# Sliding-window attention of a two-layer kernel: where in a quad the query, key and value pieces are projected and rotated

## The reference

```
h   = layernorm(x) * (1 + ca) + sa
xn  = h * rsqrt(mean(h * h) + 1e-6)
q, k, v = split(xn @ w_qkv.T)                # 16 heads of 64 each
q, k = apply_rope(q, cos, sin), apply_rope(k, cos, sin)
   # apply_rope: [x1 * c - x2 * s, x2 * c + x1 * s] on the two halves of a head
attn = softmax(where(mask, q @ k.T / 8, -1e9))   # mask: 0 <= q_pos - k_pos <= 32
x   = x + ga * ((attn @ v) @ w_out.T)
```

## Time and profile before

| what | value |
|---|---|
| median of 3 runs | 1284.41 us (1284.17 to 1285.26) |
| span of the profiled execution | 1295.1 us |
| PE busy | 975.8 us, 75% of the span |
| DVE busy | 805.3 us, 62% |
| ACT busy | 639.2 us, 49% |
| POOL busy | 430.4 us, 33% |

### The profile page before, as it was taken

The page is one execution under the profiler, slowest core; times in us unless marked ns, Lnnn a source line. Parts: engine busy times, 40 slices in busy tenths (PEclk is TensorE's granted clock), DMA queues, the critical chain, the costliest instruction groups (busy, mean ns, idle before and its releaser), DMA issues. The chain is left out here.

```text
span 1295.1 us, 25137 instructions
## 1 busy us (share of the span) xinstructions
PE 975.8 (75%) x8604; PEld 662.5 (51%) x8604; DVE 805.3 (62%) x1683; ACT 639.2 (49%) x2132; POOL 430.4 (33%) x332
## 2 busy tenths in 40 slices
PE   6779998989899999985613769747348787867665
PEld 3456565656656565664503556534225454545454
DVE  5777758687777767564657514112136878559995
ACT  3565767767676767671101323112038777643322
POOL 2334333333342423321000857886611312200221
PEclk9789899999999998987555789888759999868967
DMA  6564343434443434431402123445310000000000
GB/s 198 150 182 107 92 123 88 119 96 113 102 113 100 113 83 107 104 91 42 102 0 62 45 59 69 61 73 129 31 66 1 1 2 1 1 1 9 17 17 25
DMA packets 89009, 93.62 MB, mean 72 GB/s; under 512 B 18800, under 2 KB 62304, under 8 KB 88944
## 3 DMA queue, kind: packets, MB, share of 16 engines
q1 hardware_dynamic: 78576, 84.12, 24.7%
q0 software_dynamic: 10368, 8.66, 4.7%
HBM read 24.36 MB, written 10.70 MB: 27 GB/s over the span
## 5 line engine op out<-in xcount | busy, mean ns | idle before, releaser
L835 POOL TENSOR_TENSOR qk_cos<-qk_raw,const 128x512 f32<-128x512 f32 x128 | 183.2, 1432 | 313.0 <-ACT qk_raw L589 313.0
L575 ACT ACTIVATE prob<-psS,neg_max 128x96 f32<-128x96 f32 x512 | 167.9, 342 | 86.5 <-DVE neg_max L670 85.7
L442 PE MATMUL psQ<-a_xnT,weights 128*128 128x512 f32 x250 | 146.0, 668 | 2.1 <-ACT a_xnT L621 1.4
L550 PEld LDWEIGHTS psO<-probT,v_windows 96*64 96x64 f32 x2048 | 73.7, 143 | 142.6 <-ACT probT L649 121.1
L550 PE MATMUL psO<-probT,v_windows 96*64 96x64 f32 x2048 | 91.8, 235 | 43.9 <-ACT probT L649 43.9
L685 DVE TENSOR_TENSOR qk_roped<-qk_cos,qk_swapped 128x512 f32<-128x512 f32 x128 | 119.0, 929 | 5.9 <-DVE qk_swapped L676 5.5
L1508 POOL DMA_INDIRECT sums<-ex_y,ex_index x64 | 97.6, 1525 | 39.5 <-issue 23.5
L1497 POOL DMA_INDIRECT ex_rows<-rows,ex_index x64 | 67.1, 1048 | 121.8 <-DMA ex_index<-lists 102.6
L575 ACT ACTIVATION_READ_ACCUMULATOR prob<-psS,neg_max 128x1 f32 x512 | 105.4, 206 | 0.0
L1442 ACT ACTIVATE ex_hidden<-ex_psH,ex_b 128x512 f32<-128x512 f32 x64 | 43.7, 687 | 114.4 <-PE ex_psH L1401 59.7
L649 ACT COPY probT<-psT 96x512 f32<-96x512 f32 x128 | 76.8, 600 | 46.5 <-PE psT L530 46.5
(11 more groups left out here) (317 smaller groups left out, 1936.2 us busy)
## 6 DMA issues: line engine op xcount, KB each, us to landing
qk_swapped<-qk_raw SPq DMA_DIRECT2D x512, 64.0 KB, 2.0
v_windows<-v_tok SPq DMA_DIRECT2D x32, 384.0 KB, 4.4
v_windows<-v_tok SPq DMA_DIRECT2D x32, 256.0 KB, 3.6
mod<-mod_rows SPq DMA_DIRECT2D x12, 512.0 KB, 6.0
ex_w<-in_L_ffn_W SPq DMA_DIRECT2D x16, 256.0 KB
v_windows<-v_tok SPq DMA_DIRECT2D x32, 96.0 KB, 2.1
rows<-rt_h SPq DMA_DIRECT2D x8, 256.0 KB, 2.4
sums<-rt_zeros SPq DMA_DIRECT2D x8, 256.0 KB, 2.7
```

The lines of the kernel that those rows point to most:

```text
L442: last = nc.tensor.matmul(bank, k.wqkvT[:, col:col + P], xnT[:, :], start=True, stop=True)
L550: ins = nc.tensor.matmul(psO[D * j:D * j + D, i * P + a * HALF:i * P + (a + 1) * HALF], vw[:, par, a, t, hd], probT[:, 2 * j + i, a * HALF ...
L575: last = nc.scalar.activation(prob[:, s, 2 * j + i, :], psS[:, s, j, i * KW:(i + 1) * KW], ACT.Exp, bias=nmax[:, s, 2 * j + i:2 * j + i + ...
L835: nc.gpsimd.tensor_tensor(rcos[:, half, :], raw[:, half, :], k.const[:, K_COS:K_COS + T], ALU.mult).then_inc(cos_done, 1)
```

## The change

The six pieces of a quad are renumbered: 0 to 3 are the halves and 4 and 5 the value pieces. The plan's numbers stay, so that unit 2 now projects two halves and unit 3 two value pieces. A table, `ROPES`, says what DVE rotates: in unit 0 halves 2 and 3 of the next quad, both behind the sines of the first and the maxima, in unit 1 nothing, in units 2 and 3 as before. POOL and SP take the halves in the same order as before, with each one's wait set to its new place.

```diff
-        VALUE = (3, 5)
+        VALUE = (HALVES, HALVES + 1)
         PLAN = ((0,), (1,), (2, 3), (4, 5))
-        def half_of(m):
-            return m - m // 4
+        ROPES = (((1, 2), (1, 3)), (), ((2, 0),), ((2, 1),))
...
+        def ropes_at(u, last):
+            g, t = divmod(u, TILES)
+            return [(g + n, half) for n, half in ROPES[t] if not (last and g + n >= QUADS)]
...
                 for u in range(UNITS):
-                    t = u % TILES
-                    q, half = ahead(u, 6)
-                    roping = not (last and q >= QUADS)
+                    ropes = ropes_at(u, last)
                     if u > 0 and not (last and u + 1 >= UNITS):
                         divide(b, u + 1)
-                    if roping:
+                    for q, half in ropes[:1]:
                         done = sines(b, q, half)
-                    if t == 1 and roping:
-                        rope(b, q, half, done)
                     if not (last and u + 2 >= UNITS):
                         maxes(b, u + 2)
-                    if t != 1 and roping:
+                    for q, half in ropes[:1]:
                         rope(b, q, half, done)
+                    for q, half in ropes[1:]:
+                        rope(b, q, half, sines(b, q, half))
...
             def cosines(b, q, half):
-                first = isinstance(b, int) and b == 0 and q < 2
-                wait(pool, piece_out, b * QUADS * PIECES + q * PIECES + ((1, 2, 3, 4) if first else (1, 2, 3, 5))[half])
+                wait(pool, piece_out, b * QUADS * PIECES + q * PIECES + half + 1)
...
-                    q, half = ahead(u, 8)
-                    if not (last and q >= QUADS):
-                        swap(b, q, half)
+                    for q, m in pieces_at(g, t, last):
+                        if m not in VALUE:
+                            swap(b, q, m)
```

More of the change, by code:

```diff
@@ L357, in phase_attention0 @@
         ONTO = [psQ[:, 0, :], psQ[:, 1, :], psO[:, :]]
-        OPENING = [(0, m) for m in (0, 1, 2, 4, 3, 5)] + ["wo0", "wo1"] + [(1, m) for m in (0, 1, 2, 4, 3, 5)]
+        OPENING = [(0, m) for m in range(PIECES)] + ["wo0", "wo1"] + [(1, m) for m in range(PIECES)]
         scored, turned, applied = sem("scored"), sem("turned"), sem("applied")
@@ L391, in pieces_at @@
             return [] if last and g + 2 >= QUADS else [(g + 2, m) for m in PLAN[t]]
-        def ahead(u, n):
-            return (u + n) // HALVES, (u + n) % HALVES
+        def ropes_at(u, last):
+            g, t = divmod(u, TILES)
+            return [(g + n, half) for n, half in ROPES[t] if not (last and g + n >= QUADS)]
         def sixth_bank(n):
@@ L439, in project_onto @@
                 if m not in VALUE:
-                    half = half_of(m)
-                    col = (half % 2) * H0 * D + (2 * g + half // 2) * P
+                    col = (m % 2) * H0 * D + (2 * g + m // 2) * P
                     last = nc.tensor.matmul(bank, k.wqkvT[:, col:col + P], xnT[:, :], start=True, stop=True)
@@ L509, in _ @@
                     pe.wait_ge(w_dve, 1)
-                if OPENING[n] == (0, 3):
+                if OPENING[n] == (0, VALUE[0]):
                     pe.wait_ge(w_act, 2)
@@ L585, in piece_from @@
                 if m not in VALUE:
-                    half = half_of(m)
                     if not (isinstance(b, int) and b == 0 and q == 0):
-                        wait(act, roped, b * HALVES * QUADS + HALVES * (q - 1) + half + 1)
-                    ins = nc.scalar.copy(raw[:, half, :], bank)
+                        wait(act, roped, b * HALVES * QUADS + HALVES * (q - 1) + m + 1)
+                    ins = nc.scalar.copy(raw[:, m, :], bank)
                 else:
@@ L635, in _ @@
                 opening(n)
-                if OPENING[n] == (0, 4):
+                if OPENING[n] == (0, HALVES - 1):
                     copy_sixth(4)
@@ L843, in _ @@
             pool.wait_ge(ld_const, 16)
[L844 to L848, removed]
+            for q in range(2):
+                for half in range(HALVES):
+                    cosines(0, q, half)
             def body(b, last):
                 for u in range(UNITS):
-                    q, half = ahead(u, 7)
-                    if not (last and q >= QUADS):
-                        cosines(b, q, half)
+                    g, half = divmod(u, HALVES)
+                    if not (last and g + 2 >= QUADS):
+                        cosines(b, g + 2, half)
                     if u == 0 and isinstance(b, int) and b == 0:
@@ L867, in swap @@
             def swap(b, q, half):
-                first = isinstance(b, int) and b == 0 and q < 2
-                wait(sp, piece_out, b * QUADS * PIECES + q * PIECES + ((1, 2, 3, 4) if first else (1, 2, 3, 5))[half])
+                wait(sp, piece_out, b * QUADS * PIECES + q * PIECES + half + 1)
                 for n in range(4):
```

## The result

The changed kernel takes 1309.42 us (median; 1307.81 to 1309.57) where the kernel before takes 1284.84 beside it: ratio 1.0171, interval 1.0146 to 1.0196, slower by about 22 us (the two medians are 24.6 apart). The prediction was 1297 with a range up to 1306: right in direction, too small in size.

A forecast was written before the change was run, and what follows sets the result against it. No engine is full; waits going round between ACT, DVE and PE set a quad. Six sequences at 1.8 us (10.9), 1 for the first and 1.2 for the last give +13 us on 1284.4: 1297, range 1282 to 1306.

The forecast's parts named there:

- +0.35 into the third quad's unit 1: Delay carried through a sequence's first two quads to the third quad's unit 1, an estimate; bounds −0.4 and +1.4.
- +0.50 left in unit 0: Unit 0: part of unit 3's delay is covered by slack; exponentials start at 311.90 instead of 311.40.
- Unit 3's sines shut out: Unit 3: moved half's cosines meet the division and get in ahead of the sines; exponentials 1.02 us later.
- Two rotations in unit 0: End of unit 0: cosines shut out the first rope, two ropes queue, DVE 1.6 us late at unit 1.
- The division in unit 1: Unit 1: cosines ask 0.20 us ahead of the division and shut it out; exponentials 1.46 us later.
- the division wins: Rival in unit 1: division gets in ahead of the cosines; quad only 0.60 us longer, 1291 us; chance 0.25.
- What costs nothing: Items priced at zero: PE's 0.26 us wait for the rope goes, the late division follows; last half's swap has time.
- "worse" rival: Unit 2: a third meeting, cosines with its division, adds 0.57 us a quad; 1311 us; chance 0.05.
- first sequence: One more cosine ahead of the first sequence's loop; +1 us, bounds −1 and +3.
- six middle sequences: Each of six sequences 1.8 us longer, from +0.35 and the third quad's 1.46; 10.9 us together.
- last sequence: Last sequence, which projects in two quads only; +1.2 us.
- likeliest case: Both meetings happen, with unit 3's sines and unit 1's division shut out; 1297 us, 1292 to 1303; chance 0.45.

The follow-up runs named there:

- x4: Changed kernel with twelve dead transposes ahead of PE's wait for unit 1's division in the second and fourth quad; 1295.30 us, ratio 1.0066 to the kernel before.
- x3: Changed kernel, but POOL's cosines of the last half wait for unit 3's maxima; 1284.95 us, ratio 0.9985 to the kernel before.
- x5: Changed kernel, but POOL's cosines of half 1 wait for unit 1's division; 1292.18 us, ratio 1.0037 to the kernel before.
- x10: Kernel before with the same twelve dead transposes at the same two places; 1285.18 us, ratio 0.9996 to the kernel before.

## Why the prediction was right about the waits and wrong about the sum

**Step by step.** The table gives how much later than before the exponentials of a unit start in the fourth sequence, counted from the sequence's start (262.06 in the first profile of before, whose rows are compared here; 268.74 in the changed kernel, 263.54 in x4). The prediction's column adds its terms: +0.35 into the third quad's unit 1, +1.02 in unit 3, +0.50 left in unit 0, +1.46 in unit 1. That x4 has exactly +0.35 in the first row is luck: the prediction gives it bounds of −0.4 and +1.4 and no working.

| exponentials | predicted | changed kernel | x4, clock held |
|---|---|---|---|
| third quad, unit 1 | +0.35 | +0.79 | +0.35 |
| third quad, unit 3 | +1.37 | +1.81 | +1.38 |
| fourth quad, unit 0 | +0.85 | +1.30 | +0.87 |
| fourth quad, unit 1 | +1.81 | +2.46 | +2.04 |
| fourth quad, unit 2 | +1.81 | +3.21 | +2.04 |

*Unit 3's sines shut out: right.* 1.76 against 1.77, and the step is +1.02 in the changed kernel too (1.81 − 0.79). x3 shows the cause: with the cosines held back the sines take 0.68 and the step vanishes.

*Two rotations in unit 0: right in size, another instruction paid.* Cosines and first rope start within 0.02 of each other (319.25 and 319.27), and the rope went first: it kept its 0.68, the cosines took 1.83 and shut out the second sines (1.76) instead. I had the cosines 0.06 ahead there (311.74 against 311.8). DVE doesn't idle before unit 1's reciprocal, as predicted.

*The division in unit 1: right, by less than I thought.* I had the cosines 0.20 ahead of the division; they came 0.07 ahead. They had not to wait for the rope, ran their full 1.26 and ended 1.31 behind it, not 1.14; the division ended 0.41 behind them (322.56 + 1.26 = 323.82 against 324.23), as in the earlier trace rows. The Trainium skill, "SBUF — State Buffer", section "Who interferes with whom", says that the order of issue decides who is blocked; the trace agrees at a lead of 0.07 us, while at 0.02 us (319.25 above) the recorded starts don't tell who was first. The step is +1.67 (2.46 − 0.79) against +1.46. x5, where the division wins, has the +0.62 of that rival, and in timing it is 1.3% below the changed kernel (meeting and clock together), so the case that I took for likelier was the one that happened.

*"What costs nothing": the step that failed.* The prediction says there that PE's wait for the rope goes, "but the division is late there next", and names "PE's next transposes" among what is queued behind the late division. It gives that wait no price, as if PE only stood still for 1.9 us beside other late engines. But every projection, score and output product comes behind it on PE, and the granted clock fell to 1.2 GHz there. In the second quad, where the wait is 1.55, this happened in each middle sequence (+0.44 in the table's first row, which x4 has not); in the fourth quad, with 1.89, in every second one. There unit 2's exponentials wait no longer for maxima but for a half's copy that waits 1.45 for PE's slow projection: +0.75 (3.21 − 2.46), and the sequence ends about 1.2 later than its neighbours. x4 puts the falls at some 13.5 of the 22 us; my sum had them at nothing without a reason, and the range had no term for them and so ended below the result. The prediction's "worse" rival gave 1311, near the time, but by luck: its reason was a third meeting in unit 2, and that isn't there: in the changed kernel unit 2's division at 326.38 takes 0.56.

**The sum**, from the starts of y_mul, against the second profile of before (us):

| part | predicted | changed kernel | x4 |
|---|---|---|---|
| first sequence | +1 | +4.0 | +0.9 |
| six middle sequences | +10.9 | +16.8 | +10.5 |
| last sequence | +1.2 | +1.9 | −0.4 |
| all | +13 | +22.7 | +11.0 |

With the clock held the walk gives the middle sequences to 0.4 us, in part by luck: a middle sequence of x4 is 2.04 longer than an undisturbed one of before (70.64 against 68.60), not 1.81, but the first of the six was 69.94 before. Without, they lose another 6.3. Another 2.3 us are the last sequence's and 3.1 the first's, and in the first the share that is due to the clock is less sure: the kernel before with filler (x10) has 124.2 at its end, 2.8 more than without, so this part changes from profile to profile. Timed, x4 is 8.5 us above before (5.7 to 11.3), the changed kernel 22. The prediction's likeliest case, 1292 to 1303, is also a little narrow by its own bounds: added outright they give 1291 to 1305, which still ends below the result.

What stays open is why the clock falls in every second sequence at the same wait. The loop's code is the same for both, and PE waits 1.89 in both.

## What to carry to other kernels

A walk along the timeline that prices waits should, for each wait that it moves onto PE, give two sums: one with the clock held and one in which what stands behind the wait on PE takes its half-clock durations (here 1.74 instead of 1.12 for a projection). Where POOL's and DVE's products shut each other out as here, ask of each moved transfer which DVE instruction runs at the moment when POOL's comes; if one meeting turns on a tenth of a microsecond, a semaphore that puts POOL's work behind the critical DVE instruction is worth more than the reordering itself (from +1.7% to −1.1% by two waits). Take two profiles of the kernel before ahead of making a sum against one: here they differed by 13 us in span.

## What the runs showed of the hardware

- TensorE's granted clock fell from 2.4 to 1.2 GHz behind waits of 1.55 and 1.89 us, although PE was busy 65.13 of the sequence's 72.3 us. The Trainium skill, "TensorE: Matmul & The Clock Gate", section "A second HAM failure mode: psum-queue depth-cycling", says of a matmul kernel that frequent short pauses of PE between groups of matmuls made its clock swing between the two levels. This case's trace shows the same swing, behind single waits, and that dead transposes in the wait take it away (x4: 1.00).
- A fall need not cost anything. The kernel before, in its second profile, has four middle sequences at a mean of 0.98, each with one fall behind a PE wait of 1.47 or 1.53 us. Two of them are 68.60 and 68.67 long, as those at 1.00 (68.59 and 68.62); the other two are 68.91 and 69.94. One of the first two:

```profile
260.00:328.60 68.60, 63.96 (x743) 42.73 (x741) 49.26 (x98) 48.20 (x193) 24.22 (x17) 0.98 0.41 105
```

- Cosines that start in a free moment take 1.26; behind a rope that got in first 1.83 (319.25). DVE's instruction behind them ends 0.55 later (two inputs of 128x512, 319.87 + 1.76 against 319.25 + 1.83), and 0.41 later for the division of 128x384. Over all profiles of these runs, cosines that start 0.06 us or more ahead of such a DVE instruction go first.
